# Four chained image layers on one core: output products and additions by PSUM bank, the last transfer from ScalarE's queue

## The reference

```
x_proj = einsum('mc,bchw->bmhw', w_in, x)            # 128 channels to 16
fs     = fftshift(fft2(x_proj))                      # gain chosen by direction of the peaks
x_enh  = ifft2(ifftshift(fs * gain)).real
out    = einsum('cm,bmhw->bchw', w_out, x_enh)       # 16 channels back to 128
return x + out
```

## Time and profile before

| | |
|---|---|
| median of 3 runs | 278.42 us (278.32 to 278.46) |
| profiled execution | 278.63 us, of which the span from first to last instruction is 276.8 us |
| TensorE busy | 264.9 us, 96% of the span |
| VectorE, ScalarE, GpSimd busy | 174.3, 184.7, 63.3 us |
| granted TensorE clock | 1.000 of full speed over the span |
| transfers | 8.52 MB, output 2.10 MB in 8 transfers |

### The profile page before, as it was taken

How to read it: one execution, slowest core, us unless ns; L and a number is a source line. 1 busy time by engine, 2 the same in 40 slices (tenths; PEclk the granted TensorE clock), 3 DMA queues, 4 the chain that set the end, 5 groups by cost and what they waited for, 6 DMA issues and landing times.

```text
span 276.8 us, 4058 instructions
## 1 busy us (share of the span) xinstructions
PE 264.9 (96%) x1328; PEld 157.1 (57%) x1331; DVE 174.3 (63%) x297; ACT 184.7 (67%) x355; POOL 63.3 (23%) x97
## 2 busy tenths in 40 slices
PE   7999999999999999999999999988999998899993
PEld 2864666457655665563667535844545546664573
DVE  4686769687645743276776978777325247646773
ACT  1584477887887667665787577988846758647430
POOL 2016018300400002537821300110003607500000
PEclk9999999999999999999999999999999999999999
DMA  5990000000000010000000000000000000000026
GB/s 170 281 305 3 0 0 4 23 26 26 4 0 0 0 54 2 0 1 1 3 0 1 0 2 1 4 1 0 0 1 0 2 0 4 1 1 2 1 78 227
DMA packets 4573, 8.52 MB, mean 31 GB/s; under 512 B 1250, under 2 KB 2018, under 8 KB 4554
## 3 DMA queue, kind: packets, MB, share of 16 engines
q1 hardware_dynamic: 4554, 8.27, 9.1%
HBM read 5.60 MB, written 2.10 MB: 28 GB/s over the span
## 4 chain that ended last, share of the span: by engine, by line
PE 87%; ACT 4%; DVE 3%; DMA 2%; issue 1%; SPq 0%; DVEq 0%; ACTq 0%
PE psum L366 84%; DMA qs<-row 2%; DMA xin<-in_x 1%; PE psum L491 1%; DVE nmax L890 1%; DVE xl L852 1%; SPq L354 0%; ACT L748 0%; ACT L742 0%; ACT e L661 0%; DVE x L871 0%; ACT qs L676 0%; DVEq L199 0%; PE psum L467 0%; ACT x2T L698 0%
## 5 line engine op out<-in xcount | busy, mean ns | idle before, releaser
L366 PE MATMUL psum<-e,v 128*128 128x512 f32 x128 | 60.0, 593 | 0.0
L890 DVE TENSOR_REDUCE nmax<-psum 128x1 f32<-128x1024 f32 x32 | 38.5, 1221 | 19.6 <-PE psum L366 19.6
L661 ACT ACTIVATE e<-psum,nmax 128x1024 f32<-128x1024 f32 x32 | 35.7, 1115 | 18.0 <-issue 12.7
L861 DVE TENSOR_REDUCE nmax<-psum 128x1 f32<-128x1024 f32 x32 | 39.0, 1221 | 11.5 <-PE psum L366 10.9
L694 ACT ACTIVATE e<-psum 128x1024 f32<-128x1024 f32 x32 | 32.2, 1024 | 14.1 <-PE psum L366 13.6
L684 ACT ACTIVATE psum<-psum,nmax 128x1024 f32<-128x1024 f32 x32 | 34.9, 1091 | 8.5 <-DVE nmax L890 8.5
L366 PEld LDWEIGHTS psum<-e,v 128*128 128x128 f32 x128 | 23.7, 189 | 18.9 <-issue 15.9
L1051 POOL CAST qs<-qs 32x512 fp32r<-32x512 f32 x16 | 9.7, 606 | 102.9 <-ACT qs L676 102.1
L366 PE MATMUL psum<-qs,ks 96*128 96x512 f32 (+1 forms) x96 | 30.1, 415 | 2.4 <-DMA qs<-row 2.0
L366 PE MATMUL psum<-ks,qs 96*128 96x512 f32 (+1 forms) x96 | 31.1, 428 | 1.0 <-ACT e L694 0.7
L366 PE MATMUL psum<-e,v0n 128*64 128x512 f32 x128 | 30.9, 605 | 0.0
(11 more groups left out here) (174 smaller groups left out, 409.8 us busy)
## 6 DMA issues: line engine op xcount, KB each, us to landing
out<-xin SPq DMA_DIRECT2D x8, 256.0 KB, 2.1
xin<-in_x SPq DMA_DIRECT2D x3, 512.0 KB, 6.2
twist<-in_twist_in SPq DMA_DIRECT2D x1, 768.0 KB, 8.6
zz<-in_region_in SPq DMA_DIRECT2D x2, 360.0 KB, 6.7
xin<-in_x SPq DMA_DIRECT2D x2, 256.0 KB, 2.7
untwist<-in_untwist_in SPq DMA_DIRECT2D x1, 512.0 KB, 8.2
e<-in_near_in SPq DMA_DIRECT2D x1, 272.0 KB, 8.8
rw<-in_rows_w SPq DMA_DIRECT2D x1, 256.0 KB, 2.7
```

Source lines behind the costliest of these rows:

```text
L366: return nc.tensor.matmul(o, lhsT, rhs, start=start, stop=stop, skip_group_check=skip)
L661: inc(go(e0[:, E0_AT[b, i], :], t[:, :], ACT.Exp, bias=nmax0[z][:, i:i + 1], accum_out=sum0[z][:, i:i + 1]), "e0_ready", b)
L861: inc(vec.tensor_reduce(nmax0[z][:, i:i + 1], t[:, :], AX.X, ALU.max, negate=True), "nmax0_ready", b)
L890: inc(vec.tensor_reduce(nmax1[z][:, i:i + 1], t[:, :], AX.X, ALU.max, negate=True), "nmax1_ready", b)
```

## The change

TensorE's step i of `wout` does the four calls of the array half and PSUM bank k = i, and no longer two of each. VectorE's `y` step i adds what lies in bank i, across both image halves, and waits for `y_full` i alone. SyncE waits for the second `y_ready` of an image before it issues its transfers, both one after the other; of image 3 it issues the first half only. ScalarE has a new last step, `out.3.1`: it waits for the same event and issues the transfer of image 3's second half from its own queue.

```diff
-    "i2.2.0 i1.3.0 i2.3.0")
+    "i2.2.0 i1.3.0 i2.3.0 out.3.1")
...
             for b in range(B):
-                for h in range(2):
+                wait(sp, "y_ready", b, 1)
+                for h in range(1 if b == B - 1 else 2):
                     hc = slice(h * HALF, (h + 1) * HALF)
-                    wait(sp, "y_ready", b, h)
                     sp.dma_start(out[b][:, hc], xin[:, b, hc]).then_inc(out_written, 16)
...
-                    for j in (2 * i, 2 * i + 1):
-                        for k in range(2):
-                            half, o = slice(k * BM, (k + 1) * BM), k * HALF + j * P
-                            last = mm(t[:, o:o + P], woutT[half, j, :], xe[z][half, :], True, True)
+                    half = slice(i * BM, (i + 1) * BM)
+                    for j in range(CH // 2):
+                        o = i * HALF + j * P
+                        last = mm(t[:, o:o + P], woutT[half, j, :], xe[z][half, :], True, True)
...
-                if name == "sqrt":
+                if name == "out":
+                    wait(act, "y_ready", b, 1)
+                    act.dma_start(out[b][:, hc], xin[:, b, hc]).then_inc(out_written, 16)
+                elif name == "sqrt":
...
-                    wait(dve, "y_full", b, 1)
+                    wait(dve, "y_full", b, i)
                     wait(dve, "x3_ready", b, 1)
-                    tv = tile(("wout", b, 0)).rearrange("p (j a w) -> p a j w", j=CH, w=W)[:, 2 * i:2 * i + 2]
-                    xv = xin[:, b, hc].rearrange("p (a j w) -> p a j w", j=CH, w=W)
+                    banked = slice(i * CH // 2, (i + 1) * CH // 2)
+                    tv = tile(("wout", b, 0)).rearrange("p (j a w) -> p a j w", j=CH, w=W)[:, :, banked]
+                    xv = xin[:, b, :].rearrange("p (a j w) -> p a j w", j=CH, w=W)[:, :, banked]
                     inc(vec.tensor_tensor(xv, tv, xv, ALU.add), "y_ready", b)
```

## The result

The changed kernel takes 283.48 us (median of 4 runs, 283.19 to 283.70), the kernel before beside it 278.44; the ratio is 1.0164, with a 95% interval of 1.0118 to 1.0209. The direction was forecast, the size was not: +5.0 us where +2.4 had been worked out, outside the range. The kernel before has two groups of runs, one from 278.3 to 279.5 us and one from 280.2 to 280.9 (28 of its 105 runs in all that follows, without a single one of 1480.37 us that is left aside).

A forecast was written before the change was run, and what follows sets the result against it. TensorE's own order was taken to bound the kernel. Terms 1.76 + 0 + 0 + 0.65 = +2.41 us gave 281.04 on the profiled 278.63, or 280.8 us against the 278.42 median; range 280.15 to 282.1.

The forecast's parts named there:

- wout.2: TensorE's back-to-back steps wout.2.0 and wout.2.1: lower-half records start while upper ones wait, 16 records in 1.16 us, cost 0.
- the clock: Whole program: no term; the tail was read at full granted clock (1.00) and the sum laid on the profiled 278.63 us.
- The lone steps: TensorE's wout.0.0, wout.0.1, wout.1.0, wout.1.1: no pairing on one half, 0.44 us more each, 4 x 0.44 = +1.76 us.
- wout.3 and the additions: End of image 3: both banks complete together, y.3.0 starts at the same distance behind wout.3; cost 0.
- the rival with halves in order: TensorE's halves queue in order: +0.66 us for wout.2, +0.05 at wout.3 with its hidden addition, 281.5 us; chance 0.32.
- The transfers: Image 3's two output transfers start together after y.3.1, with no spare bandwidth: +0.65 us to the last landing.
- The queue's 0.6: Rival, dear second queue: ScalarE's transfer adds 0.6 us to either main case, 281.4 or 282.1 us; chance 0.11.
- The strides of the additions: VectorE's additions: 687 ns each, only strides change, priced at 0, bounds -0.1 and +0.1 for the last two.
- the cases that are slower: Chances: forecast 0.50, halves in order 0.32, dear queue 0.11, anything else slower 0.01; slower in all given as 0.93.

The follow-up runs named there:

- the kernel with alternating calls: Changed kernel with TensorE's calls back in alternating order, both additions waiting for the second y_full; twelve runs from 279.08 to 281.47 us, ratio 1.0024.
- the kernel with 2.05 us steps: Kernel before with calls in the changed order and those of images 0 and 1 made twice; six runs, ratio 1.0266 without the longest (293.55 us).

## Why the prediction was wrong

The forecast was +2.4 us and +5.0 were measured. Of the 2.6 us between them, 0.5 are the overlap in wout.2, and 2.0 the clock, for which the sum had no term.

*The lone steps*: right. 1.16 us for 0.72, four times, +1.76, and no wait took TensorE's place.

*wout.2*: the step that failed inside the tail. I took 0, "both halves are full again", and kept +0.66 for a strict order; it was +0.55. I had the rows for the better answer and said so: four groups of i1 prove an overtaking past three waiting records, the change needed seven. The look-ahead is bounded, so I should have worked the sum out with it. Past three, the lower half starts with the fifth upper record; three slots then hold two records, 16 - 3 = 13 slots, 5 x 0.11 = +0.55. That it is three and not four comes from the 0.21 us between a half's first two records, which no row of mine had.

*wout.3 and the additions*: 0 forecast, -0.02 measured, by other means than I had said. The order costs 0.55 and the addition under it gives 0.56 back, as in the rival with halves in order (+0.05). The TensorE page of the Trainium skill ("TensorE: Matmul & The Clock Gate", "What overlaps and what doesn't") has matmuls strictly in order. Here four records for the lower half of the array start beside upper ones only once five of eight have gone, yet at once past three waiting ones; neither its rule nor mine of full overtaking describes that.

*The transfers*: +0.65 forecast, +0.6 measured in the changed kernel and, by itself, in the kernel with alternating calls. The queue's 0.6 was none. The Trainium skill ("DMA: Bandwidth & Descriptors", "Issuing engines are not separate DMA queues") says that a second issuer only saves issue time; here the shortest runs are 281.45 beside 281.52 us, so it saved at most 0.1 us.

*The strides of the additions*: 0, as taken: 1.29 us for two, before and after.

The tail's sum with the mended term is 1.76 + 0.55 - 0.02 + 0.6 = 2.9 us, the measured tail. On an undisturbed 278.4 that is 281.3, inside the range, though nearer to the rival with halves in order (281.5) than to the forecast (280.8); the changed kernel's shortest run is 281.45. The chances contain a slip of 0.01: the cases that are slower add up to 0.94, not 0.93.

*The clock*: the step that failed by more. The sum was laid on one profiled run with a mean clock of 1.00, and the prediction took the tail's clock to stay and the rest of the program to cost what it had cost there; a term for the clock stood at nothing, and no reason was given. Measured are 2.0 us ahead of the tail, 0.35 from a late rise at the start and 1.63 at 184 us. Other runs of the kernel before do not look like the profiled one either: the wait before scoreT.2.0 leaves TensorE idle for 1 us, and a quarter of the runs are in the upper group, some 1.7 us longer. The four runs of the changed kernel first measured had the stretch, and the run of the kernel before that I argued from did not; the range had no room for it. The change is not needed for it (kernels with the old order of calls have the upper group) and does not always bring it (the changed kernel has a run at 281.45). But it came in seven of the changed kernel's ten runs, and of the kernel before only 28 of 105 are in the upper group; whether the change makes it more frequent, and why all four first runs had it, stays open. And the change has a cost that I had not on my list at all: in 9 of 33 runs of kernels with its lone steps the clock falls in the tail, for another 6 us (8 in the kernel with 2.05 us steps). With the wait filled, four of six runs have it with the lone steps in halves and none of six without them; and none of six where they are as long but use both halves, so the length alone does not bring it (these two on another chip). Against the unused half of the array as the whole cause stands the kernel with 2.05 us on one half, which had the fall in only one run of six. So the order of the lone steps brings the fall; by what it does so, and in which runs, is not shown.

## What to carry to other kernels

Where a contraction has 64 rows, alternate the calls between the two halves of the array, and look at what an order that suits another engine does to that: here one addition hidden (0.56 us) was paid with 2.9 us on TensorE (1.76 + 0.55 + 0.55). If a long queue on one part of the array can't be avoided, work out the overlap with a bounded look-ahead, three waiting records here, before forecasting full or none. One profile shows only one way in which the granted clock can go: list the idle stretches of TensorE, the 1 us wait at 181 us here, and leave room in the range for a fall of the clock behind them (1.6 to 1.7 us for this one).

## What the runs showed of the hardware that was not expected

With these fp32 matmuls of 64 rows, TensorE started a record for the free half of the array past three that waited for the busy half, and not past more: 0.72 us for 8 records with four and four, 1.71 us for 16 with eight and eight. The granted clock fell from 1.00 to 0.50 with TensorE busy 3.10 of 3.10 and 3.60 of 3.60 us by its records, when these used one half of the array. The Trainium skill ("TensorE: Matmul & The Clock Gate", "Part 1: The HAM clock gate") ties the lower clock to an idle engine. The stretch at 184 us fits that in part, since it stands behind a wait of 1.02 us; the fall in the tail does not, with no wait over 0.17 us from 262 us on. Four matmuls on one bank, each waiting for the one before, added some 0.4 us, though 1.0 us of waiting had seemed free.
